# Filler products in the openings of two attentions, and a shorter first lot on GpSimd

## The chip, the cores and the metric

One NeuronCore of one Trainium2 chip. The metric is the device time of one execution of the program in microseconds; the time of a kernel is the median of several executions.

## What is computed

A block of two layers on 2048 tokens of 128 float32 numbers, `x` of shape (2, 1024, 128):

```python
x = x + attn0(layernorm(x))   # 16 heads of 8, 4 key/value heads, full attention over 1024, plus a state-space scan and a gated FFN
x = x + moe0(layernorm(x))    # 8 experts, 2 per token
x = x + attn1(layernorm(x))   # 16 heads on a shared latent of 32, causal over 1024
x = x + moe1(layernorm(x))    # integrator with shared and routed experts, 2 steps
...
scores = jnp.einsum('bhqd,bhkd->bhqk', q, k) / jnp.sqrt(jnp.float32(hd))
attn = jax.nn.softmax(scores, axis=-1)
attn = jnp.einsum('bhqk,bhkd->bhqd', attn, v)
```

Filler products write only into scratch banks of PSUM that are overwritten later, so they change no result.

## The kernel before, in words

One function, `attention` (line 141), builds both attentions. It is called with a "front" object that threads other work of its layer through it: `HybridFront` (line 642) for the first, a causal one for the second. The work is cut into 8 units of 4 heads and one batch each. For every unit two passes run over the scores:

- the **max pass**: 32 steps (`max_unit`, line 366) of 128 queries x one head. TensorE writes the scores of up to 1024 keys into two banks as bf16 quads, a quad (`quad`, line 359) being four products of 32 columns side by side, line 362. VectorE takes the row maximum (`take_max`, line 573: line 581 for the full, line 578 for the causal attention). Two pairs of banks alternate, so TensorE is at most two steps ahead of VectorE. In the causal attention the steps grow from 128 to 1024 keys.
- the **exp pass**: slots `s` (32 for the full, 24 for the causal attention), each with two exp quads (`exp_unit`, line 393), two exponentials on ScalarE (line 528) and, in every second slot, products with v (`pv_quad`, line 413, line 425).

Between them the maxima of half a unit are negated and split into three bf16 parts by five small operations on VectorE (`combine`, lines 591 to 595), turned on TensorE (`turn_max`, line 388), copied by ScalarE (`rows`, line 514) and sent by three DMAs on SyncE's queue into the operand of the exp quads (line 310). The exp pass of a unit runs in the same slots as the max pass of the next; a table computed from costs (`places`, lines 206 to 224) sets which max step stands in which half slot.

The first unit has nothing before it to share slots with. So `attention` begins with an **opening**: the first `own_from` max steps of unit 0 alone (21 in the full attention, 30 in the causal one), with the front's own products between them (`front.tensor_second`), the combine after step 15 on VectorE, the transposes `turn_max(0, 0)` after step 17 on TensorE, and then slot 0 of the body. To these steps TensorE adds fillers (`filler`, line 451): one bf16 quad of a 128x128 identity over 512 columns. In the full attention they follow steps 8 to 20, in the causal one steps 24 to 29, and eight more stand in slots 1 to 3 and 6 to 10 of the causal body.

Meanwhile GpSimd makes 96 products ahead for the scan that follows the first attention (`HybridFront.gpsimd_third`, line 743: the product of line 759, then its DMA, line 762). They come in lots: before product 7, 13, 19 and so on, GpSimd waits until the next combine of VectorE is done (`mparts_ready`).

In the trace, tiles bear the names of the memory they lie in: `banks` are PSUM banks, `attn_ka` and `attn_qa` the keys and queries, `attn_identb` the bf16 identity, `attn_mx` to `attn_mparts` the maxima and their parts. ScalarE's line 528 writes the probabilities, two of whose four buffers are borrowed and appear as `centred_squares`.

Of the kernel before, what the change touches and what calls it, by code (L numbers as in the profile page):

```python
# [140 lines left out]
def attention(k, tag, q_lin, k_lin, k_heads, v, causal, attn_t, front, units, tok=None, residual=False,  # L141
# [6 lines left out]
    nc = k.nc  # L148
# [11 lines left out]
    with ExitStack() as ctx:  # L160
# [18 lines left out]
        scores_exp = [k.bank[4], k.bank[5]]  # L179
        out_acc = k.bank[6]  # L180
        turned = k.bank[7]
# [25 lines left out]
        first_half = sum(1 for u in max_units if u[0] < QT // 2)  # L207
        joined = [COMBINE if causal and n in (first_half - 1, NM - 1) else 0 for n in range(NM)]
        whole = sum(cost) + sum(joined)
        own_from = min(n for n in range(NM + 1) if sum(cost[n:]) * reached[NE] <= sum(cost) * reached[DUE + 1])  # L210
        stream = [(0, n) for n in range(own_from, NM)] + [(1, n) for n in range(own_from)]
        places, done, spent = [], 0, 0
        for place in range(2 * NE):
            upto = done
            share = reached[place // 2] + weight[place // 2] * (1 + place % 2) / 2
            while upto < NM and spent + cost[stream[upto][1]] / 2 <= whole * share / reached[NE]:
                n = stream[upto][1]
# [24 lines left out]
        mrow_ready = [k.sem(f"{tag}_mrow_ready{h}") for h in range(2)]  # L242
# [26 lines left out]
        with nc.Block() as block:  # L269
# [85 lines left out]
            def _(pe):  # L355
# [3 lines left out]
                def quad(out, lhs, rhs, start=True):  # L359

                    for t in range(4):
                        last = nc.tensor.matmul(out[sl(t, 32), :], lhs[:, sl(t, 32)], rhs, start=start, stop=True,  # L362
                                                skip_group_check=True)
                    return last
# [48 lines left out]
                def pv_quad(i, kt_slot, vstage, part):  # L413

                    qb, kt, _, c0 = exp_units[kt_slot]
                    if part == 0:
                        pe.wait_ge(probs_ready, 2 * (NE * i + kt_slot + 2))
                        if kt_slot == 0:
                            pe.wait_ge(vstaged, i + 1)
                        if kt_slot == 0 or kt_slot == MID:  # L420
                            pe.wait_ge(osb_ready, 2 * i + qb)
                    mid = (c0 + BLK) // 2
                    cols = slice(c0, mid) if part == 0 else slice(mid, BLK)
                    for j in range(4):
                        last = nc.tensor.matmul(out_acc[32 * j:32 * j + 32, cols], vstage[:, kt, kj(j), :],  # L425
                                                probs[(kt_slot + j // 2) % 4][:, j % 2, cols],

                                                start=kt == 0 and part == 0,
                                                stop=kt_slot + 1 == half_end[qb], skip_group_check=True)
                    if part == 1:  # L430
                        last.then_inc(pv_done, 2)

                def turn_out(i, qb):

                    pe.wait_ge(osb_ready, 2 * i + qb + 1)
                    pe.wait_ge(normed, 2 * i + qb)

                    if qb == 0:
                        pe.wait_ge(mrow_ready[1], i + 1)
                    elif i + 1 < UNITS:  # L440
                        pe.wait_ge(mrow_ready[1 if causal else 0], i + 2)
                    for t in range(4):
                        last = quad(turned[:, sl(t, TILE)], osb[:, sl(t, TILE)], k.m("ident"))
                    last.then_inc(oturned, 1)

                def first_pass(i, place):
                    for ahead, n in places[place]:
                        if i + ahead < UNITS:
                            max_unit(i + ahead, n)

                def filler(bank):
                    quad(bank, ident_b[:, :], ident_b[:, :].unsqueeze(1).to_broadcast([128, 4, 128]))

                def body(i):
                    for s in range(NE):
                        odd = s % 2 == 1
                        if causal and i == 0 and s in (1, 2, 3, 6, 7, 8, 9, 10):
                            pe.wait_ge(mrow_ready[0 if s < 6 else 1], 1)
                            filler(turned[:, :])
                        if odd and s > 1:  # L460
                            products_with_v = (i, s - 3, vst[i % 2])
                        elif odd and i > 0:
                            products_with_v = (i - 1, NE - 2, vst[1 - i % 2])
                        else:
                            products_with_v = None
                        if products_with_v:
                            pv_quad(*products_with_v, 0)
                        exp_unit(i, s, (0,))
                        first_pass(i, 2 * s)
                        exp_unit(i, s, (1,))  # L470
                        if s == turn_at[1]:
                            turn_max(i, 1)
                        if s == turn_at[0] and i + 1 < UNITS:
                            turn_max(i + 1, 0)
                        first_pass(i, 2 * s + 1)
                        if products_with_v:
                            pv_quad(*products_with_v, 1)
                        if s == OUT_AT and i > 0:
                            turn_out(i - 1, 1)
                        if s == MID + 3:  # L480
                            turn_out(i, 0)
# [3 lines left out]
                for n in range(own_from):  # L485
                    max_unit(0, n)
                    front.tensor_second(pe, n)
                    if n >= (own_from - 6 if causal else 8):
                        filler(scores_exp[0][:, :])
                    if n == first_half + 1:  # L490
                        turn_max(0, 0)
                for i in range(UNITS):
# [149 lines left out]
class HybridFront:  # L642
# [100 lines left out]
    def gpsimd_third(self, pool):  # L743

        nc, scan = self.k.nc, self.scan
        pool.wait_ge(self.part_ready[0][2], 3)
        pool.wait_ge(self.part_ready[1][2], 3)
        n = 0
        for b in range(2):
            for jj in range(D // 16):  # L750
                for m in AHEAD_UNITS:
                    if n >= 7 and n % 6 == 1:
                        pool.wait_ge(self.mparts_ready[(n // 6 - 1) % 2], (n // 6 + 1) // 2)
                    channel = 32 * (m % 4) + 4 * jj + m // 4
                    stage, kept = self.stage[n % 2], self.kept[n % 2]
                    if n >= 2:
                        pool.wait_ge(kept, 16 * (n // 2))
                    x = scan.x_turned[:, 8 * b:8 * b + 8, channel:channel + 1].to_broadcast([128, 8, TILE])
                    nc.gpsimd.tensor_tensor(stage[:, :, :], scan.b_turned[:, 8 * b:8 * b + 8, :], x, ALU.mult)\  # L759
                        .then_inc(self.made_ahead, 1)  # L760
                    pool.wait_ge(self.made_ahead, n + 1)
                    pool.dma_start(self.d["ahead"][n], stage[:, :, :]).then_inc(kept, 16)
                    n += 1
        for i in range(2):
            pool.wait_ge(self.kept[i], 16 * (n // 2))
# [2479 lines left out]
```

## Time and profile before

| | before |
|---|---|
| median of 3 runs | 1913.61 us (1909.39 to 1915.45) |
| profiled execution | 1912.95 us |
| its span in the profile | 1911.1 us |
| mean granted clock of TensorE | 0.919 |
| TensorE matmul busy | 1649.7 us (86%) |
| VectorE busy | 1478.6 us (77%) |
| ScalarE busy | 1350.1 us (71%) |
| GpSimd busy | 888.5 us (46%) |

The span runs from the first to the last instruction on the core; the profiled execution's own time has 1.85 us more around it. The first attention with its front takes roughly the stretch from 60 to 520 us, its opening begins at 108; the scan with the first MoE follows; the second attention's opening begins near 1287. The granted clock is the share of TensorE's full clock, 2.4 GHz, that was given in a stretch: 1.00 is 2.4 GHz, 0.50 is 1.2 GHz, and a number between them is a mean over both. Durations of products in the trace include the way through the array after the last column, so the time from one start to the next is what a product costs on TensorE.

### The profile page before, as it was taken

How to read it: one execution, taken by the hardware profiler on the slowest of the kernel's cores; microseconds unless marked ns; L12 is line 12 of the kernel's file. 1: busy time of each engine (PE TensorE's matmuls, PEld its weight loads, DVE VectorE, ACT ScalarE, POOL GpSimd, SP SyncE). 2: the span in 40 equal slices, each digit the busy share in tenths (PEclk: the TensorE clock that was granted, in tenths of full speed). 3: DMA queues.
4: the chain of work that ended last, by engine and by line, in shares of the span. 5: the costliest groups of instructions: out<-in, count | busy, mean ns of one | idle time of the engine just before them, and what ended most of it. 6: DMA issues, size and time to landing. Idle time of an engine off the chain costs nothing. (4 is left out here: it accounts for less than half of the span.)

```text
span 1911.1 us, 45999 instructions
## 1 busy us (share of the span) xinstructions
PE 1649.7 (86%) x17410; PEld 874.4 (46%) x17422; DVE 1478.6 (77%) x1729; ACT 1350.1 (71%) x2673; POOL 888.5 (46%) x572
## 2 busy tenths in 40 slices
PE   6789999999788877777777669998999998999996
PEld 2235555555344444444444433433656556344442
DVE  3688899999299999999999975447888845556457
ACT  4417888888799999989999953443777773654443
POOL 1165666666099999999999981000000002000000
PEclk8858999999998888898888889996999999999998
DMA  2343444443489898888888942021222100000000
GB/s 117 123 160 139 157 154 161 159 153 141 141 312 315 314 315 298 311 279 292 302 322 296 305 150 88 12 73 42 47 37 45 29 4 18 1 1 0 0 6 17
DMA packets 82504, 278.86 MB, mean 146 GB/s; under 512 B 11159, under 2 KB 11954, under 8 KB 81311
## 3 DMA queue, kind: packets, MB, share of 16 engines
q1 hardware_dynamic: 68223, 225.67, 35.6%
q0 software_dynamic: 13824, 50.34, 6.8%
q8 instruction: 124, 2.03, 0.5%
q10 hardware_dynamic: 288, 0.45, 0.1%
q14 instruction: 45, 0.37, 0.1%
HBM read 214.72 MB, written 61.21 MB: 144 GB/s over the span
## 5 line engine op out<-in xcount | busy, mean ns | idle before, releaser
L1664 POOL TENSOR_TENSOR hc<-st,ct 128x1024 f32<-128x1024 f32 x256 | 598.2, 2374 | 8.2 <-DVE st L1623 7.7
L1623 DVE TENSOR_TENSOR_SCAN st<-da,banks 128x1024 f32<-128x1024 f32 x256 | 562.5, 2265 | 17.3 <-ACT da L1580 7.2
L528 ACT ACTIVATE attn_probs<-banks 128x512 f32<-128x512 f32 (+3 forms) x640 | 324.9, 534 | 93.3 <-PE banks L362 76.7
L362 PE MATMUL banks<-attn_qa,attn_ka 75*32 75x512 bf16 (+3 forms) x3584 | 347.9, 365 | 9.1 <-DMA attn_qa<-attn_mrow 2.8
L581 DVE TENSOR_REDUCE attn_mx<-banks 128x1 f32<-128x1024 f32 x256 | 309.8, 1223 | 32.7 <-PE banks L362 20.5
L1588 ACT ACTIVATE ut<-b_turned,mats 128x128 f32<-128x128 f32 x1024 | 311.7, 387 | 1.7
L362 PE MATMUL banks<-attn_ka,attn_qa 72*32 72x512 bf16 (+3 forms) x3584 | 291.3, 381 | 17.9 <-DVE attn_mx L578 11.0
L1580 ACT ACTIVATE da<-dt,mats 128x1024 f32<-128x1024 f32 x256 | 282.3, 1138 | 27.2 <-DVE st L1623 19.3
L1505 PE MATMUL banks<-hc,onecol 128*32 128x512 f32 x1024 | 159.5, 699 | 93.6 <-POOL onecol L1662 73.6
L759 POOL TENSOR_TENSOR made_ahead<-b_turned,x_turned 128x1024 f32<-128x1024 f32 x96 | 184.0, 1916 | 93.4 <-DVE attn_mparts L595 72.1
L578 DVE CUSTOM_DVE_ANT_0 banks<-banks,attn_maskwide 128x128 f32<-128x128 f32 (+7 forms) x256 | 191.1, 775 | 31.8 <-PE banks L362 28.4
L1481 PE MATMUL banks<-mats,ut 128*128 128x128 f32 x1024 | 177.4, 307 | 37.5 <-DVE st L1623 21.5
L425 PE MATMUL banks<-attn_probs,attn_vst 128*32 128x256 f32 (+3 forms) x2560 | 180.9, 350 | 1.6 <-ACT attn_probs L528 0.5
L528 ACT ACTIVATE centred_squares<-banks 128x512 f32<-128x512 f32 x256 | 150.6, 596 | 39.0 <-PE banks L362 29.5
L1481 PEld LDWEIGHTS banks<-mats,ut 128*128 128x128 f32 x1024 | 137.5, 154 | 80.4 <-ACT ut L1588 48.2
L362 PEld LDWEIGHTS banks<-attn_qa,attn_ka 75*32 75x32 bf16 x3584 | 101.5, 95 | 133.2 <-ACT attn_probs L528 47.6
L1489 PEld LDWEIGHTS banks<-mats,ua 128*128 128x128 f32 x768 | 104.7, 167 | 106.3 <-issue 66.9
L362 PEld LDWEIGHTS banks<-attn_ka,attn_qa 72*32 72x32 bf16 x3584 | 108.3, 99 | 98.1 <-DVE attn_mx L578 23.7
L2609 PE MATMUL banks<-hid_m,ew 128*128 128x512 f32 x320 | 146.5, 592 | 0.5
L1489 PE MATMUL banks<-mats,ua 128*128 128x128 f32 x768 | 131.0, 326 | 6.8 <-DVE st L1623 6.5
L3048 POOL MEMSET route_tok<- 128x128 bf16 x1 | 0.2, 204 | 274.5 <-issue 274.5
L425 PEld LDWEIGHTS banks<-attn_probs,attn_vst 128*32 128x32 f32 x2560 | 78.5, 110 | 34.3 <-issue 5.2
(445 smaller groups left out, 1953.3 us busy)
## 6 DMA issues: line engine op xcount, KB each, us to landing
dt<-dt_rows SPq DMA_DIRECT2D x256, 512.0 KB, 5.6
ahead<-made_ahead POOLq DMA_DIRECT2D x96, 512.0 KB, 3.5
ua<-ahead SPq DMA_DIRECT2D x96, 512.0 KB, 5.9
attn_qa<-q_lin SPq DMA_DIRECT2D x144, 64.0 KB
attn_ka<-k_lin SPq DMA_DIRECT2D x72, 64.0 KB
moe_w<-in_moe_w SPq DMA_DIRECT2D x2, 2048.0 KB, 9.8
mats<-in_mats SPq DMA_DIRECT2D x1, 2988.5 KB, 13.1
xparts_kept<-xparts_lin SPq DMA_DIRECT2D x3, 512.0 KB, 3.7
```

Of the source, the lines that this page charges most:

```text
L362: last = nc.tensor.matmul(out[sl(t, 32), :], lhs[:, sl(t, 32)], rhs, start=start, stop=True, skip_group_check=True)
L425: last = nc.tensor.matmul(out_acc[32 * j:32 * j + 32, cols], vstage[:, kt, kj(j), :], probs[(kt_slot + j // 2) % 4][:, j % 2, cols],  star ...
L528: nc.scalar.activation(probs[s % 4][:, jj, c0:BLK], scores_exp[jj][:, c0:BLK], ACT.Exp, scale=scale).then_inc(probs_ready, 1)
L578: nc.vector.tensor_tensor_reduce(out, out, mask_wide[:, SEQ - w:SEQ], 1.0, -BIG, ALU.add, ALU.max, mx[:, qt, j:j + 1]).then_inc(max_taken, 1)
L581: nc.vector.reduce_max(mx[:, qt, j:j + 1], out, AX.X).then_inc(max_taken, 1)
L759: nc.gpsimd.tensor_tensor(stage[:, :, :], scan.b_turned[:, 8 * b:8 * b + 8, :], x, ALU.mult)\
L1481: ins = nc.tensor.transpose(pair[:, i // 4, sl(i % 4, TILE)], buf[:, i, :], k.m("ident"))
L1489: ins = nc.tensor.transpose(pair[:, i // 4, sl(i % 4, TILE)], ua[q % 3][:, i, :], k.m("ident"))
L1580: nc.scalar.activation(da[n % 4][:, :], dt[n % 4][:, :], ACT.Exp, scale=a_now[:, g, jp:jp + 1])\
L1588: nc.scalar.activation(ut[TURNED.index(n) % 2][:, i, :], b_turned[:, 8 * b + i, :], ACT.Copy, scale=x_now[:, i, g, jp:jp + 1]).then_inc(ut ...
L1623: nc.vector.tensor_tensor_scan(st[n % 4][:, :], da[n % 4][:, :], pair[:, :, :].rearrange("p h t -> p (h t)"), 0.0, ALU.mult, ALU.add).then ...
L1664: nc.gpsimd.tensor_tensor(hc[n % 8][:, :], st[n % 4][:, :], ct[:, b * SEQ:(b + 1) * SEQ], ALU.mult)\
```

## The change

It has two parts.

*Fillers.* A new `wide_filler` is one float32 product: stationary the 128x128 identity, moving 256 columns (the identity twice), into one bank. In the first opening it follows each of the steps 1 to 20 (20 wide fillers), where before bf16 fillers followed steps 8 to 20 (13 of them); four more stand at the head of slots 0, 1, 2 and 4 of unit 0, behind a wait for ScalarE's first copy of the rows. In the second opening wide fillers follow the odd steps below 16 (8 of them) and all steps from 20 to 29 (10, behind the same kind of wait), where before bf16 fillers followed steps 24 to 29; the eight bf16 fillers of the causal body stay.

*GpSimd's lots.* The first lot has five products instead of seven, so each later lot begins two products earlier, and one more lot, of one product, stands at the end.

```diff
+                def wide_filler(bank):
+                    nc.tensor.matmul(bank[:, 0:256], k.m("ident"), k.m("ident").unsqueeze(1).to_broadcast([128, 2, 128]),
+                                     start=True, stop=True)
+
                 def body(i):
                     for s in range(NE):
                         odd = s % 2 == 1
                         if causal and i == 0 and s in (1, 2, 3, 6, 7, 8, 9, 10):
                             pe.wait_ge(mrow_ready[0 if s < 6 else 1], 1)
                             filler(turned[:, :])
+                        if not causal and i == 0 and s in (0, 1, 2, 4):
+                            pe.wait_ge(mrow_ready[0], 1)
+                            wide_filler(turned)
...
                 for n in range(own_from):
                     max_unit(0, n)
                     front.tensor_second(pe, n)
-                    if n >= (own_from - 6 if causal else 8):
-                        filler(scores_exp[0][:, :])
+                    if causal:
+                        if n < first_half and n % 2 == 1:
+                            wide_filler(turned)
+                        if n >= first_half + 4:
+                            pe.wait_ge(mrow_ready[0], 1)
+                            wide_filler(turned)
+                    elif n >= 1:
+                        wide_filler(scores_exp[0])
                     if n == first_half + 1:
                         turn_max(0, 0)
...
                 for m in AHEAD_UNITS:
-                    if n >= 7 and n % 6 == 1:
-                        pool.wait_ge(self.mparts_ready[(n // 6 - 1) % 2], (n // 6 + 1) // 2)
+                    if n >= 5 and n % 6 == 5:
+                        pool.wait_ge(self.mparts_ready[n // 6 % 2], n // 12 + 1)
```

Lines behind the new function are 13 higher than before.

The order of TensorE's instructions around the transposes of the first opening, before (`banks_1` and `banks_3` are the score banks of the max steps, `banks_5` those of the exp quads, `banks_7` the bank of the transposes; `x8` is two quads, that is one max step):

```order
L388 MATMUL banks_7<-attn_identb,attn_mparts 12x128 x4
L362 MATMUL banks_1<-attn_ka,attn_qa 32x512 x8
L362 MATMUL banks_5<-attn_identb 32x512 x4
L362 MATMUL banks_3<-attn_ka,attn_qa 32x512 x8
L362 MATMUL banks_5<-attn_identb 32x512 x4
L362 MATMUL banks_1<-attn_ka,attn_qa 32x512 x8
L362 MATMUL banks_5<-attn_identb 32x512 x4
L362 MATMUL banks_5<-attn_qa,attn_ka 32x512 x4
L362 MATMUL banks_3<-attn_ka,attn_qa 32x512 x8
L362 MATMUL banks_5<-attn_qa,attn_ka 32x512 x8
L362 MATMUL banks_1<-attn_ka,attn_qa 32x512 x8
```

and now:

```order
L388 MATMUL banks_7<-attn_identb,attn_mparts 12x128 x4
L362 MATMUL banks_1<-attn_ka,attn_qa 32x512 x8
L455 MATMUL banks_5<-mats 128x256
L362 MATMUL banks_3<-attn_ka,attn_qa 32x512 x8
L455 MATMUL banks_5<-mats 128x256
L362 MATMUL banks_1<-attn_ka,attn_qa 32x512 x8
L455 MATMUL banks_5<-mats 128x256
L455 MATMUL banks_7<-mats 128x256
L362 MATMUL banks_5<-attn_qa,attn_ka 32x512 x4
L362 MATMUL banks_3<-attn_ka,attn_qa 32x512 x8
L362 MATMUL banks_5<-attn_qa,attn_ka 32x512 x4
L455 MATMUL banks_7<-mats 128x256
```

A wide filler (line 455, on `mats`, where the float32 identity lies) stands in each place of a bf16 filler; one more stands in front of the first exp quad and one in front of slot 1, and slots 2 and 4 follow likewise. Ahead of this piece the wide fillers follow steps 1 to 7 too, where there was nothing.

TensorE in the second opening, from step 22 on, before:

```order
L362 MATMUL banks_1<-attn_ka,attn_qa 32x512 x4
L362 MATMUL banks_1<-attn_ka,attn_qa 32x256 x4
L362 MATMUL banks_3<-attn_ka,attn_qa 32x512 x4
L362 MATMUL banks_3<-attn_ka,attn_qa 32x256 x4
L362 MATMUL banks_1<-attn_ka,attn_qa 32x512 x4
L362 MATMUL banks_1<-attn_ka,attn_qa 32x384 x4
L362 MATMUL banks_5<-attn_identb 32x512 x4
L362 MATMUL banks_3<-attn_ka,attn_qa 32x512 x4
```

and now:

```order
L362 MATMUL banks_1<-attn_ka,attn_qa 32x512 x4
L362 MATMUL banks_1<-attn_ka,attn_qa 32x256 x4
L455 MATMUL banks_7<-mats 128x256
L362 MATMUL banks_3<-attn_ka,attn_qa 32x512 x4
L362 MATMUL banks_3<-attn_ka,attn_qa 32x256 x4
L455 MATMUL banks_7<-mats 128x256
L362 MATMUL banks_1<-attn_ka,attn_qa 32x512 x4
L362 MATMUL banks_1<-attn_ka,attn_qa 32x384 x4
```

The fillers begin four steps earlier, behind step 20, and each is one product on `banks_7` instead of four on `banks_5`.

GpSimd's products and DMAs where the second lot begins, with what they wait for, before (the row with two waits is the eighth product; the seven above it are the first lot, the last two of which stand here):

```order
L759 TENSOR_TENSOR made_ahead<-b_turned,x_turned 128x1024 [waits ahead_kept1]
L762 DMA ahead<-made_ahead 128x1024 [waits front_made_ahead]
L759 TENSOR_TENSOR made_ahead<-b_turned,x_turned 128x1024 [waits ahead_kept0]
L762 DMA ahead<-made_ahead 128x1024 [waits front_made_ahead]
L759 TENSOR_TENSOR made_ahead<-b_turned,x_turned 128x1024 [waits ahead_kept1,attn0_mparts_ready0]
L762 DMA ahead<-made_ahead 128x1024 [waits front_made_ahead]
```

and now (the row with two waits is the sixth product, the first lot has the five above it):

```order
L772 TENSOR_TENSOR made_ahead<-b_turned,x_turned 128x1024 [waits ahead_kept1]
L775 DMA ahead<-made_ahead 128x1024 [waits front_made_ahead]
L772 TENSOR_TENSOR made_ahead<-b_turned,x_turned 128x1024 [waits ahead_kept0]
L775 DMA ahead<-made_ahead 128x1024 [waits front_made_ahead]
L772 TENSOR_TENSOR made_ahead<-b_turned,x_turned 128x1024 [waits ahead_kept1,attn0_mparts_ready0]
L775 DMA ahead<-made_ahead 128x1024 [waits front_made_ahead]
```

The wait for the first combine has moved from the eighth product to the sixth; nothing else in GpSimd's order moved.

## Rows read from the trace of the kernel before

**Rows 1.** Busy time by stretch: from:to us, busy us (instructions) per engine, granted clock, DMA.

```profile
120.00:140.00 20.00, 15.73 (x148) 5.15 (x144) 19.39 (x22) 0.82 (x2) 16.96 (x13) 0.50 0.53 204
140.00:160.00 20.00, 20.00 (x228) 8.23 (x224) 12.34 (x11) 11.60 (x21) 10.65 (x9) 0.60 0.33 133
160.00:180.00 20.00, 19.45 (x376) 11.79 (x364) 18.14 (x22) 16.93 (x31) 12.66 (x11) 1.00 0.45 142
...
1280.00:1300.00 20.00, 14.00 (x79) 3.88 (x78) 12.89 (x38) 5.28 (x9) 0.00 (x0) 0.73 0.00 1
1300.00:1320.00 20.00, 16.70 (x148) 6.74 (x148) 14.82 (x35) 4.45 (x8) 4.58 (x4) 0.59 0.21 81
1320.00:1340.00 20.00, 19.95 (x408) 11.73 (x404) 15.41 (x52) 12.18 (x27) 0.00 (x0) 0.75 0.13 24
```

**Rows 2.** PE in order of time, first opening: start us, us, line, tiles, idle before.

```profile
108.25 1.90 PE L362 MATMUL banks<-attn_ka,attn_qa 72*32 72x512 bf16 x16
...
118.66 0.64 PE L362 MATMUL banks<-attn_identb 128*32 128x512 bf16 x4
119.09 1.07 PE L362 MATMUL banks<-attn_ka,attn_qa 72*32 72x512 bf16 x8
119.94 0.64 PE L362 MATMUL banks<-attn_identb 128*32 128x512 bf16 x4
...
134.62 0.59 PE L388 MATMUL banks<-attn_identb,attn_mparts 128*12 128x128 bf16 x4 [3.22 <-DVE attn_mparts L595]
...
139.69 0.65 PE L362 MATMUL banks<-attn_qa,attn_ka 75*32 75x512 bf16 x4
```

**Rows 3.** PE in order of time, second opening.

```profile
1296.56 0.62 PE L362 MATMUL banks<-attn_ka,attn_qa 72*32 72x512 bf16 x4
1297.11 2.07 PE L1838 MATMUL banks<-attn_t,mats 32*128 32x512 f32 x2
1299.11 1.04 PE L362 MATMUL banks<-attn_ka,attn_qa 72*32 72x512 bf16 x8
...
1305.21 2.08 PE L1845 MATMUL banks<-hn,lat_fold 128*128 128x512 f32 x2
1307.08 1.92 PE L1846 MATMUL banks<-hn,lat_wkv 128*128 128x512 f32 x2
1308.78 1.49 PE L1848 MATMUL banks<-lat_wkv,hn 128*128 128x128 f32 x8
```

**Rows 4.** DVE in order of time, first opening; last row: a later combine.

```profile
128.47 1.22 DVE L581 TENSOR_REDUCE attn_mx<-banks 128x1 f32<-128x1024 f32 x1
129.72 1.80 DVE L591 TENSOR_SCALAR attn_mneg<-attn_mx 128x16 f32<-128x16 f32 x1
...
131.97 2.38 DVE L594 CAST attn_mparts<-attn_mres 128x16 bf16<-128x16 f32 x1
134.39 0.17 DVE L595 TENSOR_TENSOR attn_mparts<-attn_mres,attn_mparts 128x16 bf16<-128x16 f32 x1
...
482.67 0.17 DVE L591 TENSOR_SCALAR attn_mneg<-attn_mx 128x16 f32<-128x16 f32 x1
```

**Rows 5.** POOL in order of time: products and DMA issues of the first opening.

```profile
126.74 1.90 POOL L759 TENSOR_TENSOR made_ahead<-b_turned,x_turned 128x1024 f32<-128x1024 f32 x1 [0.17 <-DMA ahead<-made_ahead]
...
129.56 1.92 POOL L759 TENSOR_TENSOR made_ahead<-b_turned,x_turned 128x1024 f32<-128x1024 f32 x1
...
132.40 1.92 POOL L759 TENSOR_TENSOR made_ahead<-b_turned,x_turned 128x1024 f32<-128x1024 f32 x1
...
163.10 1.90 POOL L759 TENSOR_TENSOR made_ahead<-b_turned,x_turned 128x1024 f32<-128x1024 f32 x1 [10.87 <-DVE attn_mparts L595]
```

**Rows 6.** ACT in order of time, first slots of the body.

```profile
140.39 0.60 ACT L528 ACTIVATE centred_squares<-banks 128x512 f32<-128x512 f32 x1 [4.56 <-PE banks L362]
...
156.44 1.19 ACT L528 ACTIVATE attn_probs<-banks 128x512 f32<-128x512 f32 x2 [0.53 <-PE banks L362]
157.75 2.50 ACT L528 ACTIVATE centred_squares<-banks 128x512 f32<-128x512 f32 x4
```

## The prediction

> **What bounds the kernel now.** I read the stretches of 20 us first, then the engines in order of time at the two openings. In the steady body of the first attention TensorE is busy 19.45 of 20 us at a granted clock of 1.00 [rows 1], so a delay or a gain in an opening is carried whole to the end of that attention, and the next stages follow. The change acts only in the two openings, where the clock is at the lower of its two levels (1.2 GHz; full is 2.4): 0.50 in 120 to 140 us, 0.60 in 140 to 160, and 0.59 and 0.75 in 1300 to 1340 [rows 1].
>
> In the first opening a max unit begins at 108.25; a unit is 0.85 us at 1.2 GHz (119.09 to 119.94) and a bf16 filler 0.43 (118.66 to 119.09) [rows 2]. Their sum, 1.28, is almost the 1.25 that VectorE needs for a take (128.47 to 129.72) [rows 4], so the two engines keep step and today's fillers are nearly free. Then TensorE stands idle 3.22 us before the transposes of line 388, which wait for the combine [rows 2]. That combine lasts from 129.72 to 134.56. Two of its five small operations took 1.80 and 2.38 us where the same operation took 0.17 at 482.67 [rows 4]. Both ended within 0.05 us of the end of a GpSimd product (129.56 and 132.40, 1.92 each) [rows 5]. The first exp quad starts at 139.69, 5.07 after the transposes [rows 2]; the exps then run at 1.2 GHz until 156.44 [rows 6].
>
> **The price of a wide filler.** No row shows a single 128x256 float32 product between two 32-column quads, so I bound it. Its stream: L1845 to L1846 is 1.87 for two passes of 512 columns, the start of which is dearer by 0.16 than L1846's (durations 2.08 and 1.92), thus 0.85 per 512 columns and 0.85 for two passes of 256 [rows 3]. Its switches: a quad of 0.43 is followed by L1838 after 0.55 (+0.12); from L1838 to the next quad it is 2.00 against the 1.71 of two undisturbed passes (+0.29) [rows 3]. Sum at 1.2 GHz: 0.85 + 0.41 = 1.26. The lower end is 0.85, if the switches hide; no row shows a full-width product hiding them, so I take 1.26. At full clock the stream halves to 0.43 and the switches lie between 0.21 and 0.41: about 0.74.
>
> **Does the clock rise?** This decides the sign. For: it rose while the full-width float32 products L1845, L1846 and L1848 ran back to back (0.59 over 1300 to 1320 mixes both levels) [rows 1, 3]. Against: from 118.66 to 130 TensorE ran units and full-array bf16 fillers with almost no gap, a third of the time in the fillers, and the clock stayed at 0.50; from 140 to 156 it was busy 20.00 of 20 us and rose only as the exps reached 156.44, when float32 products with v were in the mix [rows 1, 2, 6]. In the new opening a period is 0.85 of unit and 1.26 of wide, of which 0.41 streams nothing: per 2.11 us, 0.85 of full-array columns, 0.85 of the unit's 72 rows and 0.41 empty. The nearest row is the bf16 mixture, 0.43 of full array to 0.85 of unit with nothing empty, and it did not raise the clock. I take: it stays at 1.2 GHz through the first opening, and rises, as before, in the eighth slot or so.
>
> The Trainium skill ("TensorE: Matmul & The Clock Gate", section "Why this matters for your kernels") says that keeping TensorE busy without gaps is what brings the full clock; by it the wide fillers, which close every gap, would bring it at once, which is the first rival below. The trace does not agree with it as it stands: 140 to 156 had no gap and stayed low [rows 1, 6].
>
> **First opening, summed.** Unit 0, then units 1 to 17 each with a wide: 108.25 + 0.85 + 17 x 2.11 = 145.0, where the transposes can start, against 134.62. VectorE now waits for TensorE: its sixteenth take follows unit 15, whose quads end at 108.25 + 0.85 + 15 x 2.11 - 1.26 = 139.5; with 0.3 of hand-over and 1.25 it ends near 141, and the combine, five operations of 0.17 with their hand-overs, about 1.05, near 142. That is before 145, so **GpSimd's shorter lot gives nothing here**: the fifth product ended at 128.64 [rows 5], the sixth now waits for the combine, and what it saves (1.80 + 2.38 - 2 x 0.17 = 3.8) lies beside TensorE. The later lots move by two members and cost nothing: GpSimd already waited 10.87 before the second lot [rows 5], and the last product, now behind the combine at 482.67 [rows 4], is the last that the scan reads. Then the transposes (4 x 128 columns, 0.43), three units with wides (6.33) and the wide of slot 0 (1.26): 145.0 + 8.0 = 153.0 for the first exp quad, against 139.69: +13.3. The rows on SyncE's queue had 5.07 us before and have 8.0 now, so they are there; the new wait for the row copy in front of that wide is met, and what queues behind it waits for the landing anyway. Slots 1, 2 and 4 add 3 x 1.26 = 3.8, TensorE having no idle time there. Sum **+17.1**. With switches at half price (1.06 per wide): 17 x 0.20 + 3 x 0.20 + 4 x 0.20 less, +12.3; hidden wholly, +7.4.
>
> **Second opening.** Eight wides stand among units 0 to 15: 8 x 1.26 = 10.1 at most, beside 6.0 us of TensorE's idle time in 1280 to 1300 and 3.3 in 1300 to 1320 [rows 1]. Most is hidden; I estimate +2.5 (0 to 6), since the idle time is not all where they stand. After L1848, at the raised clock, units 20 to 29 with wides need 0.43 + 0.74 = 1.17 at most each, no more than a take. There the full clock is likely to hold, as it is TensorE half idle that lost it before, and the mean of 0.75 over 1320 to 1340, that is 10 us at 1.2 GHz with TensorE full [rows 1], becomes full clock. That halves some 9 us, of which ACT's 0.6 per exp [rows 6] leaves 3.5. Sum **-1**; ends -5, and +11 if the clock falls again and ten wides cost 1.26 each.
>
> **Forecast:** 1912.95 (the profiled execution: span 1911.1 and 1.85 around it; the median of the runs is 0.66 above it) + 17.1 - 1 = **1929**; own range 1915 to 1936.
>
> **Rivals.**
> 1. *The wides raise the clock early.* Float32 at full width may weigh otherwise than a bf16 group; no row excludes that. If it rises within the first few units and holds, unit and wide take 0.43 + 0.74 = 1.17, under a take's 1.25. VectorE sets the pace as before, the combine starts near 130 and the shorter lot pays its 3.8 in full. The fourteen exps from 140.39 to 156.44, 16.05 us, go at 0.625 each (four in 2.50 at 157.75) [rows 6]: 8.75 plus four wides of 0.74: -4.3. Two units at low clock cost 2 x 0.86 = 1.7. Sum -6.4, the second opening -4: **1902.5**, between 1898 and 1907. It decides from the unit at which the clock rises: each one at 1.2 GHz loses 2.11 - 1.25 = 0.86, so the gain of 8.1 is gone after nine, near 128 us.
> 2. *It rises between that and the transposes*: 0 to +8 in the first opening and -4 in the second, 1909 to 1917, about **1914**.
> 3. *The wides are nearly free and the clock stays*, so that only the lot acts. TensorE's 3.22 of idle time would be the gain, **1910**; but 0.85 + 0.85 is already 0.45 above a take for seventeen units, 7.7 us, which eats it. I give it no more than 0.03.
>
> **How the numbers follow.** Forecast 0.53, rival 1 0.33, rival 2 0.11, rival 3 0.03. Within 0.3% (5.7 us), about what a measurement of this kernel tells from no change, lie rivals 2 and 3 almost whole; the forecast's own low end touches that band, which the rest of rival 2 balances. So faster 0.33, same 0.13, slower 0.54. The range must take in rival 1 and most of the forecast: 1898 to 1934.
>
> **What would show it.** Right: the granted clock stays 0.50 from 108 to 153 us, unit and wide follow each other every 2.1 us, the transposes come near 145 without idle time of TensorE before them, all five operations of the combine take 0.2 us, and the clock is full from 1310. Wrong: a granted clock of 1.00 before 128 us, with takes 1.25 apart and the transposes near 131.

## The result and the profile after

The changed kernel takes 1928.93 us (median of 13 runs) against 1910.31 of the kernel before (13 runs): ratio **1.0102, 95% interval 1.0083 to 1.0121**. By the medians it is slower by 18.6 us. One of its 13 runs took 2634.93 us, at a mean granted clock of 0.554; the ratio leaves that run out, and the median of the other twelve is 1927.39. The profiled execution took 1932.9 us with a span of 1931.1, against 1911.1 before. The mean granted clock of the whole span, 0.925 against 0.919, does not show where the time went; the stretches do.

The stretches of 20 us (columns as in [rows 1]) show the first opening at 0.50 from end to end, and longer; the clock of the second opening is at 0.79 and 1.00 where it had been at 0.59 and 0.75 [rows 1], on stretches that now lie some 19 us later:

```profile
120.00:140.00 20.00, 20.00 (x99) 5.87 (x98) 12.06 (x14) 0.24 (x1) 8.90 (x8) 0.50 0.41 154
140.00:160.00 20.00, 20.00 (x106) 6.82 (x102) 10.91 (x14) 2.37 (x4) 11.95 (x9) 0.50 0.27 106
160.00:180.00 20.00, 20.00 (x192) 7.85 (x192) 9.45 (x8) 9.27 (x17) 3.11 (x3) 0.55 0.13 53
...
1320.00:1340.00 20.00, 19.29 (x149) 7.45 (x149) 15.30 (x36) 4.34 (x8) 4.58 (x4) 0.79 0.21 81
1340.00:1360.00 20.00, 19.32 (x474) 11.72 (x478) 17.93 (x61) 14.54 (x32) 0.00 (x0) 1.00 0.15 25
```

In the first two rows the profile shows no idle time of TensorE (a wide is shown 1.22 us long and the next product starts 1.15 after it, so durations overlap and a short stretch without a stream does not appear as idle), and VectorE has fallen from 19.39 [rows 1] to 12.06: TensorE now sets the pace, at the lower clock. TensorE in order of time, where [rows 2] stood:

```profile
110.62 1.90 PE L362 MATMUL banks<-attn_ka,attn_qa 72*32 72x512 bf16 x16
112.44 1.22 PE L455 MATMUL banks<-mats 128*128 128x256 f32 x2
113.59 1.04 PE L362 MATMUL banks<-attn_ka,attn_qa 72*32 72x512 bf16 x8
114.57 1.22 PE L455 MATMUL banks<-mats 128*128 128x256 f32 x2
...
146.47 1.22 PE L455 MATMUL banks<-mats 128*128 128x256 f32 x2
147.62 0.38 PE L388 MATMUL banks<-attn_identb,attn_mparts 128*12 128x128 bf16 x2
...
155.25 0.62 PE L362 MATMUL banks<-attn_qa,attn_ka 75*32 75x512 bf16 x4
```

From one wide filler to the next it is 2.13 us (112.44 to 114.57); the wide itself with its entry and first-pass price is 1.15 (112.44 to 113.59), and the step behind it takes 0.98 to the next wide in place of 0.85. The transposes stand at 147.62 without idle time before them, where they had waited 3.22 us. VectorE at the combine, where [rows 4] stood:

```profile
142.34 1.23 DVE L594 TENSOR_REDUCE attn_mx<-banks 128x1 f32<-128x1024 f32 x1 [0.90 <-PE banks L362]
143.60 0.17 DVE L604 TENSOR_SCALAR attn_mneg<-attn_mx 128x16 f32<-128x16 f32 x1
...
144.23 0.17 DVE L607 CAST attn_mparts<-attn_mres 128x16 bf16<-128x16 f32 x1
144.44 0.17 DVE L608 TENSOR_TENSOR attn_mparts<-attn_mres,attn_mparts 128x16 bf16<-128x16 f32 x1
```

The takes now wait 0.90 us each for TensorE. The combine has lost its two long operations (1.80 and 2.38, now 0.17 each), but it ends at 144.61, three microseconds ahead of the transposes that need it. ScalarE, where [rows 6] stood:

```profile
155.93 0.60 ACT L541 ACTIVATE centred_squares<-banks 128x512 f32<-128x512 f32 x1 [7.10 <-PE banks L362]
...
168.34 0.60 ACT L541 ACTIVATE centred_squares<-banks 128x512 f32<-128x512 f32 x1 [1.88 <-PE banks L362]
...
178.50 1.91 ACT L541 ACTIVATE centred_squares<-banks 128x512 f32<-128x512 f32 x3 [0.67 <-PE banks L362]
```

These are the first, the ninth and the seventeenth exp of the body. The ninth stood here in the kernel before:

```profile
148.98 0.60 ACT L528 ACTIVATE centred_squares<-banks 128x512 f32<-128x512 f32 x1 [0.61 <-PE banks L362]
```

The clock rises at 178.2, with the seventeenth; before it rose at 156.0, with the fifteenth [rows 6].

Where the 19.96 us between the two spans lie: the first step begins 2.36 later, which is not the change (nothing ahead of it is touched, and in the profiles of this study it begins anywhere from 108.25 to 111.60). From the first step to an exp of the second unit (exp 104; these numbers count from 0, and a unit has 64) it takes 131.54 us against 113.06: **+18.48**. From the first step of the second opening to its exp 40 (from 0 again) it takes 63.92 against 66.12: **-2.20**. The rest of the program is 1064.46 us between these two pieces and 559.25 behind them before, 1062.13 and 562.90 after, with the same instructions: -2.33 and +3.65, such as also lie between kernels that differ in the openings alone. Sum 2.36 + 18.48 - 2.20 - 2.33 + 3.65 = 19.96.

TensorE in the second opening: behind the full-width block of the latent's products the clock has risen, and the single wides keep it:

```profile
1324.72 2.07 PE L1858 MATMUL banks<-hn,lat_fold 128*128 128x512 f32 x2
...
1329.36 0.51 PE L362 MATMUL banks<-attn_ka,attn_qa 72*32 72x512 bf16 x8
1329.80 0.70 PE L455 MATMUL banks<-mats 128*128 128x256 f32 x2
1330.43 0.51 PE L362 MATMUL banks<-attn_ka,attn_qa 72*32 72x512 bf16 x8
```

A step of 768 keys with its wide takes 1.07 us here (1329.80 to 1330.87, the next wide), where the kernel before had fallen back to 1.2 GHz from 1313 to 1330. Earlier in this opening the single wides did not keep it: TensorE came in at full clock, and the clock fell at 1314.8, behind this wait:

```profile
1312.42 0.35 PE L362 MATMUL banks<-attn_ka,attn_qa 72*32 72x384 bf16 x4 [2.16 <-DVE attn_mx L591]
1312.70 0.70 PE L455 MATMUL banks<-mats 128*128 128x256 f32 x2
```

### The profile page after: what moved, and what is told of

Same layout as the page of the kernel before. It is cut to its first block and busy times, and to the rows that moved or that the text cites. A ratio compares the mean times of both kernels' runs of the same rounds, so it can differ in the third digit from the quotient of the medians.

```text
span 1931.1 us, 46028 instructions
## 1 busy us (share of the span) xinstructions
PE 1662.0 (86%) x17430; PEld 875.7 (45%) x17430; DVE 1476.2 (76%) x1729; ACT 1350.1 (70%) x2673; POOL 888.2 (46%) x572
## 5 line engine op out<-in xcount | busy, mean ns | idle before, releaser
L362 PE MATMUL banks<-attn_qa,attn_ka 75*32 75x512 bf16 (+3 forms) x3584 | 347.4, 364 | 10.9 <-DMA attn_qa<-attn_mrow 4.1
L362 PE MATMUL banks<-attn_ka,attn_qa 72*32 72x512 bf16 (+3 forms) x3584 | 285.8, 375 | 10.6 <-DVE attn_mx L591 6.4
L1494 PE MATMUL banks<-mats,ut 128*128 128x128 f32 x1024 | 163.3, 299 | 40.5 <-DVE st L1636 30.9
L1494 PEld LDWEIGHTS banks<-mats,ut 128*128 128x128 f32 x1024 | 131.7, 150 | 75.5 <-ACT ut L1601 48.7
```

The source lines that it names most:

```text
L1494: ins = nc.tensor.transpose(pair[:, i // 4, sl(i % 4, TILE)], buf[:, i, :], k.m("ident"))
```

## The experiments

The theory: a single wide product between two groups of 32-column products costs two switches, 0.4 us in which nothing streams, and so it makes the step dearer and does not raise the clock; everything else follows. The rivals: column groups beside the steps never raise it; the type decides; full width itself is at fault; GpSimd's lot matters. The ratios are to the kernel before, measured beside each experiment on the same chip; the experiments ran on three chips, so times are compared only where the text says that the chip is the same.

**1. Two bf16 groups in place of the wide product** (g_bf16). The stream is as long, 0.85 us at 1.2 GHz, without a switch.

```diff
 def wide_filler(bank):
-    nc.tensor.matmul(bank[:, 0:256], k.m("ident"), ident twice, start=True, stop=True)
+    for _ in range(2):
+        filler(bank[:, :])
```

> The changed kernel, but each wide filler is two bf16 groups of 32-column products over 512 columns: the same 0.85 us of stream at 1.2 GHz, with no switch to full width. Theory (the clock stayed low since 0.41 us of each 2.13 us streamed nothing): step and filler take 1.71 us, TensorE is without a gap, the granted clock becomes 1.00 within some 7 us of the first fillers and holds; the combine starts near 130 us after a first step at 108, the shorter lot pays its 3 us, and the time is 8 to 13 us under the kernel before (ratio 0.993 to 0.996). Rival A (bf16 groups beside the steps never raise it, as in the kernel before): a step and filler of 1.71 us for the whole opening, 7 us later in the first opening and about 3 more in the body, ratio 1.003 to 1.006. Rival B (float32 counts for more than bf16): as rival A here, but not in the float32 groups.

Measured: 0.9953 (0.9933 to 0.9974), 1898.31 us. TensorE in order of time, first opening:

```profile
113.28 1.07 PE L362 MATMUL banks<-attn_identb 128*32 128x512 bf16 x8
114.14 1.07 PE L362 MATMUL banks<-attn_ka,attn_qa 72*32 72x512 bf16 x8
...
116.70 0.76 PE L362 MATMUL banks<-attn_identb 128*32 128x512 bf16 x8
117.30 0.60 PE L362 MATMUL banks<-attn_ka,attn_qa 72*32 72x512 bf16 x8
117.73 0.60 PE L362 MATMUL banks<-attn_identb 128*32 128x512 bf16 x8
```

Step and filler follow each other without loss (113.28, 114.14); in the third filler the clock rises, at 117.0, 5.4 us behind the first step, and stays. The transposes come 22.17 us behind the first step, against 37.01 with the wides and 26.37 before. The expectation's rival A, that such groups never raise the clock, falls.

**2. One float32 group of 32-column products** (g_f32).

```diff
-    nc.tensor.matmul(bank[:, 0:256], k.m("ident"), ident twice, start=True, stop=True)
+    quad(bank[:, 0:256], k.m("ident"), ident twice)
```

> The changed kernel, but each wide filler is one group of four float32 products of 32 columns over 256 columns: the same type and the same 0.85 us of stream, with no switch to full width. Theory: as the bf16 groups, clock at 1.00 early in the first opening, ratio 0.993 to 0.996. Rival A (only full-width products raise it, as those of lines 1845 to 1848 did): clock at 0.50 through the first opening, ratio 1.003 to 1.006. Rival B (float32 counts for more): rises here and not with bf16 groups.

Measured: 0.9940 (0.9920 to 0.9961), 1897.77 us. TensorE in order of time:

```profile
114.00 1.07 PE L362 MATMUL banks<-mats 128*32 128x256 f32 x8
114.85 1.07 PE L362 MATMUL banks<-attn_ka,attn_qa 72*32 72x512 bf16 x8
115.71 1.07 PE L362 MATMUL banks<-mats 128*32 128x256 f32 x8
116.56 0.65 PE L362 MATMUL banks<-attn_ka,attn_qa 72*32 72x512 bf16 x8
```

The clock rises at 116.6, 6.0 us behind the first step, and the transposes come after 22.33. The two types do the same. A second measurement, with more rounds:

> The kernel with float32 groups of 32 columns once more, with more rounds, beside its variations. Theory: ratio 0.992 to 0.996, clock at 1.00 some 7 us behind the first step.

Again 0.9940 (0.9920 to 0.9960), 1897.49 us. This kernel is faster than the kernel before and than the changed one.

**3. Two bf16 products of full width** (w_bf16): the switches, with the other type.

```diff
-    nc.tensor.matmul(bank[:, 0:256], k.m("ident"), ident twice, start=True, stop=True)
+    for _ in range(2):
+        nc.tensor.matmul(bank[:, :], ident_b[:, :], ident_b four times, start=True, stop=True)
```

> The changed kernel, but each wide filler is two bf16 products of full width, 128x128 by 512 columns: the same stream of 0.85 us at 1.2 GHz and the same switches at both sides. Theory: the switches cost much the same as with float32, step and filler near 2.1 us (2.0 if the first pass's share of 0.16 belongs to float32), the clock stays at 0.50 and the time is that of the changed kernel within 5 us, ratio 1.006 to 1.011. Rival B (the type decides, float32 being too weak or too dear): the clock rises, ratio under 1.000.

Measured: 1.0035 (1.0010 to 1.0061), 1912.56 us, between the two answers and below the range that the theory gave. TensorE in order of time:

```profile
112.78 1.03 PE L456 MATMUL banks<-attn_identb 128*128 128x512 bf16 x2
113.75 1.04 PE L362 MATMUL banks<-attn_ka,attn_qa 72*32 72x512 bf16 x8
114.72 1.03 PE L456 MATMUL banks<-attn_identb 128*128 128x512 bf16 x2
...
150.04 1.86 PE L456 MATMUL banks<-attn_identb 128*128 128x512 bf16 x4
151.83 0.40 PE L362 MATMUL banks<-attn_qa,attn_ka 75*32 75x512 bf16 x4
```

Step and filler take 1.94 us: the switches cost 0.12 on either side (0.97 each for 0.85 of stream), and the 0.16 of the first pass is float32's. The clock stays at 0.50 for the whole opening, as the theory says; but it rises at 151.75, where two fillers stand in a row before the first exp quad, and the body runs at full clock from its first slot. That, and 20 steps at 0.19 us less, is the distance to the changed kernel.

**4. Four wides in a row behind steps 1 and 2, single ones behind the rest** (wide_start): full width, float32, but less switching at the start.

```diff
 elif n >= 1:
-    wide_filler(scores_exp[0])
+    for _ in range(4 if n <= 2 else 1):
+        wide_filler(scores_exp[0])
```

> The changed kernel, but after steps 1 and 2 of the first opening stand four wide fillers in a row instead of one; the single ones after steps 3 to 20 stay. Theory (it is the share of the time without a stream, not the full width or the type, that keeps the clock low; at full clock single wides are enough to hold it): the clock becomes 1.00 within 10 us of the first step and stays so; a step with its single wide then takes no longer than a take; 5 us are lost at the start, 11 us won later; ratio 0.994 to 0.998. Rival (full-width products between column groups never carry the clock): it rises during the eight and falls again within some us, or does not rise; ratio over 1.010.

TensorE in order of time:

```profile
110.87 3.78 PE L455 MATMUL banks<-mats 128*128 128x256 f32 x8
114.58 0.62 PE L362 MATMUL banks<-attn_ka,attn_qa 72*32 72x512 bf16 x8
115.13 1.99 PE L455 MATMUL banks<-mats 128*128 128x256 f32 x8
...
117.60 0.70 PE L455 MATMUL banks<-mats 128*128 128x256 f32 x2
118.23 0.61 PE L362 MATMUL banks<-attn_ka,attn_qa 72*32 72x512 bf16 x8
118.77 0.70 PE L455 MATMUL banks<-mats 128*128 128x256 f32 x2
```

The clock rises at 114.6, at the end of the first four, and the single wides then hold it through the opening and the body, at 1.17 us for step and wide (117.60 to 118.77). So full width carries the clock, and the change's own pattern of the first opening holds it here once it is up; in the change it did not raise it. The time is a miss: 1.0005 (0.9989 to 1.0021), not 0.994 to 0.998. In the profiled execution, 1902.53 us, the lowest of the ten, it is 107.2 us from the first step to exp 104, against 113.1 before. A clock that rises later in the other executions is not the likely reason: the mean granted clock of the whole span was 0.940 in the profiled one, 0.933 to 0.941 in all ten, and 0.916 to 0.931 in the kernel before on this chip. Part of the miss may lie in what it is compared with: experiment 9 has the first opening of before and the second of the change, and in its profile the same way takes 110.5 us. On the same chip its kernel took 1908.79 us and this one 1905.67, 3.1 less, with 3.3 less on that way. Why neither is under the kernel before stays open.

**5. Half the length, without a switch** (g_half).

```diff
-    quad(bank[:, 0:256], k.m("ident"), ident twice)
+    quad(bank[:, 0:128], k.m("ident"), k.m("ident"))
```

> The kernel with float32 groups of half the length: four products of 32 columns over 128 columns, 0.43 us at 1.2 GHz, everywhere. Theory (it takes enough stream, as the kernel before shows with bf16 fillers of the same 0.43): the clock stays at 0.50 in the first opening until the products with v, as in the kernel before; step and filler 1.28; with the shorter lot the time is 0 to 4 us under before, ratio 0.998 to 1.000. Rival (any float32 group raises it): clock at 1.00 early, ratio 0.992 to 0.996.

Measured: 0.9993 (0.9974 to 1.0013). TensorE in order of time:

```profile
113.57 0.64 PE L362 MATMUL banks<-mats 128*32 128x128 f32 x8
114.00 1.07 PE L362 MATMUL banks<-attn_ka,attn_qa 72*32 72x512 bf16 x8
114.85 0.64 PE L362 MATMUL banks<-mats 128*32 128x128 f32 x8
```

From 113.57 to 127.0 step follows filler without a gap, at 1.28 us (later the trace shows 0.39 and 0.23 us of idle time), and the clock stays at 0.50 until 148.7, among the products with v. So TensorE without gaps for 13 us did not raise it, in float32 as little as in the kernel before with bf16; with twice the filler it rose (experiments 1 and 2). Empty time is therefore not the whole account: here there was none, and half the filler.

**6. GpSimd's shorter lot alone** (lot5).

```diff
-                    if n >= 7 and n % 6 == 1:
-                        pool.wait_ge(self.mparts_ready[(n // 6 - 1) % 2], (n // 6 + 1) // 2)
+                    if n >= 5 and n % 6 == 5:
+                        pool.wait_ge(self.mparts_ready[n // 6 % 2], n // 12 + 1)
```

> The kernel before with GpSimd's shorter first lot alone. Theory (the combine on the path only while TensorE keeps step with VectorE, as it does in the kernel before): the five operations of the combine take 0.17 us each, the transposes start near 131.3 instead of 134.62, and the time falls by about 3 us (ratio 0.998 to 0.9985). Rival (the shorter lot gives nothing anywhere, because the copy and landing of the rows end later than TensorE's own work): the transposes come earlier, the first exp quad does not, ratio 1.000.

Measured: 0.9986 (0.9969 to 1.0004), 1906.21 us: at the upper edge of what the theory named, with an interval that also holds 1, so the time does not show the gain. VectorE in order of time:

```profile
130.88 0.17 DVE L591 TENSOR_SCALAR attn_mneg<-attn_mx 128x16 f32<-128x16 f32 x1
...
131.50 0.17 DVE L594 CAST attn_mparts<-attn_mres 128x16 bf16<-128x16 f32 x1
```

The transposes come 22.93 us behind the first step in place of 26.37, the first exp 28.85 in place of 32.13: -3.3, as the theory has it, and not the rival's zero. But how much the old lot costs differs from one execution to the next. In the profile of experiment 9, which has the old lot in the same opening, one operation of the combine is long and not two:

```profile
132.32 0.18 DVE L602 CAST attn_mparts<-attn_mneg 128x16 bf16<-128x16 f32 x1
132.53 2.44 DVE L603 TENSOR_TENSOR attn_mres<-attn_mneg,attn_mparts 128x16 f32<-128x16 f32 x1
```

There the transposes come after 24.82 us and the first exp after 30.59, and the shorter lot is worth 1.7. In the profiled execution of this experiment the clock rose only at 169.7, six slots later than before, with the same order of work, which hid the gain there. With the mixture of the kernel before that moment differs between profiles: it came 43.9 us behind the first step in experiment 9, 47.7 before and 60.3 here. What sets it no run shows.

**7. Seven products with the float32 groups** (g_f32_lot7), against experiment 2:

```diff
-                    if n >= 5 and n % 6 == 5:
-                        pool.wait_ge(self.mparts_ready[n // 6 % 2], n // 12 + 1)
+                    if n >= 7 and n % 6 == 1:
+                        pool.wait_ge(self.mparts_ready[(n // 6 - 1) % 2], (n // 6 + 1) // 2)
```

> The kernel with float32 groups, but GpSimd's first lot of seven products as before. Theory (at full clock VectorE sets the pace, so a combine stretched by products 6 and 7 is on the path): two of the combine's operations take about 1.9 us again, the transposes come some 3 us later behind the first step than the 22.3 us with five products, ratio 0.9935 to 0.998, 2 to 3 us above the kernel with five. Rival (TensorE's units and fillers cover it): the transposes come at the same place and the time is the same.

Measured: 0.9950 (0.9930 to 0.9971), 1898.85 us, 1.4 above its twin with five on the same chip; the intervals do not part them. TensorE, with the stretch that the combine leaves it idle, and 2 us windows of the same place:

```profile
133.42 0.39 PE L388 MATMUL banks<-attn_identb,attn_mparts 128*12 128x128 bf16 x4 [1.87 <-DVE attn_mparts L607]
134.68 1.05 PE L362 MATMUL banks<-attn_ka,attn_qa 72*32 72x512 bf16 x8 [0.87 <-DVE attn_mx L593]
```

```profile
132.00:134.00 2.00, 0.39 (x4) 0.20 (x4) 1.93 (x3) 0.15 (x1) 1.70 (x2) 1.00 0.43 176
134.00:136.00 2.00, 1.32 (x16) 0.57 (x20) 1.98 (x3) 0.42 (x1) 1.63 (x2) 0.64 0.65 264
...
142.00:144.00 2.00, 2.00 (x44) 0.99 (x36) 1.92 (x2) 1.79 (x3) 1.21 (x2) 1.00 0.32 129
```

One operation of the combine took 1.93 us, and the transposes came 1.2 us later (23.57 behind the first step), not 3: a miss in size. But more was lost in another way. The clock fell at 134.5 and came back at 141.4, and the first exp is 3.2 to 3.9 us later than in the two profiles with five products (31.47 against 27.60 and 28.27).

**8. The first opening's wides alone, with those of the first body's slots** (first_only), against the change, with the old lot as in experiment 7:

```diff
                     if causal:
-                        if n < first_half and n % 2 == 1:
-                            wide_filler(turned)
-                        if n >= first_half + 4:
-                            pe.wait_ge(mrow_ready[0], 1)
-                            wide_filler(turned)
+                        if n >= own_from - 6:
+                            filler(scores_exp[0][:, :])
```

> The kernel before with the wide fillers of the first opening and its body alone; GpSimd's lot of seven and the second opening as before. Theory (the loss is the first opening at 1.2 GHz, and the shorter lot is hidden there): from the first step to the first exp 45.3 us as in the changed kernel (32.1 before), clock at 0.50 until behind the fourth slot, products 6 and 7 of GpSimd harmless because the combine begins 10 us later. About 17 to 20 us above before, ratio 1.009 to 1.0105. Rival (the shorter lot matters, in the sense that without it the combine is stretched on the path): 3 us more than the changed kernel, ratio over 1.0115.

Measured: 1.0104 (1.0079 to 1.0129), 1927.59 us (four runs); 45.31 us from the first step to the first exp, the same as in the changed kernel. Within these intervals the whole loss is the first opening, and the lot changes nothing in it: all five operations of the combine take under 0.18 us here with the old lot too.

**9. The second opening's wides alone** (second_only), against the change, with the old lot and without the wides in the first body's slots:

```diff
-                    elif n >= 1:
-                        wide_filler(scores_exp[0])
+                    elif n >= 8:
+                        filler(scores_exp[0][:, :])
```

> The kernel before with the wide fillers of the second opening alone. Theory (there the full-width block of lines 1845 to 1848 raises the clock and the wide fillers from step 20 hold it): the fall of the clock at 1313 to 1330 us is gone; from the first step of that opening to its exp 40 it takes some 2 to 3 us less than the 66.1 of before, ratio 0.9985 to 0.999. Rival (no net gain, the eight odd fillers cost what the clock gives): ratio 1.000, the interval across 1.

Measured: 1.0007 (0.9984 to 1.0031), the value of the rival. In the profile the way from the first step of the second opening to its exp 40 takes 63.61 us against 66.12: 2.5 less, as the theory has it, and too little for the runs to show.

**10. No fillers in the first body** (g_f32_nobody, and once more nobody_again), against experiment 2:

```diff
-                        if not causal and i == 0 and s in (0, 1, 2, 4):
-                            pe.wait_ge(mrow_ready[0], 1)
-                            wide_filler(turned)
```

> The kernel with float32 groups of 32 columns as fillers, without the four fillers in slots 0, 1, 2 and 4 of the first body. Theory (at full clock the body's own products keep it; TensorE is the bound there): four times 0.43 us less, some 1 to 1.7 us under the kernel with them, ratio to before about 0.993 to 0.994. Rival (the first slots have no products with v and cannot hold the clock): it falls between the first exp quad and slot 4 and comes back later, ratio 0.996 or more.

> The same without the four fillers in the first body's slots, once more with more rounds. If these fillers only cost time at full clock: 1 to 1.7 us under the kernel with them; if they are needed to hold the clock in some executions: the same or more. Ratio to before 0.992 to 0.996.

Measured: 0.9959 (0.9939 to 0.9980) and 0.9954 (0.9934 to 0.9973), not under experiment 2 (0.9940, twice); on the chip where both were measured it took 1900.48 us against 1897.49. In both profiles the clock holds without them, and the seventeenth exp comes 0.3 to 1.1 us earlier behind the first step (38.19 and 38.07 against 38.52 and 39.20). The expected gain of 1 to 1.7 us is not there in the time, and why not stays open.

## Why the prediction was right, point by point

*The size* was right: 1929 forecast, 1928.93 measured. That it fits to a tenth is luck: the forecast added 16.1 us to a profiled execution that lay 2.6 over the median of the larger number of runs, the two profiled executions differ by 19.95 and the medians by 18.6, and two terms were off in opposite directions.

*The price of a wide*, 1.26 us by the sum of stream, entry, first pass and exit, was right: a step with its wide was forecast at 2.11 and takes 2.13. So was the price at full clock, which no row showed: forecast 1.17 for a step of 1024 keys with its wide, and 1.17 in experiment 4.

*The clock stays low* was right, and the ground for it held up. The row that decided it was the nearest one, the bf16 mixture that had not raised the clock, and the empty 0.41 us that made the wide mixture thinner, not denser. Experiments 1 and 2 keep the stream and take the switches away, the 0.41 us with them, and the clock rises in 6 us; experiment 3 keeps them with the other type, and it stays low. That full width as such is not at fault is shown by experiment 4, where four wides in a row raise it. What is not shown apart is the empty time from the alternation itself: no run puts column groups beside the steps with an idle time of 0.4 us between them. The changed kernel shows TensorE busy 20.00 of 20 us at 0.50, and in experiment 5 it runs for 13 us without a gap at 0.50 too. The rule of the Trainium skill ("TensorE: Matmul & The Clock Gate", section "Why this matters for your kernels"), that a TensorE kept busy without gaps gets the full clock, does not hold here as it stands.

*The first opening*: transposes forecast 36.75 us behind the first step (145.0 less 108.25), measured 37.01; first exp quad +13.3 us against before, measured 44.64 less 31.44, +13.2; the three wides in slots 1, 2 and 4 forecast +3.8, measured +3.8 (by the profiles' own times the ninth exp is 19.36 late, the first 15.54). The sum was 17.1 and came out 18.5: what it missed is that the clock rose one slot later, which cost 1.4 more. It had been set to come "as before, in the eighth slot or so".

*GpSimd's lot gives nothing here*: right (experiment 8), since the combine ends three microseconds ahead of the transposes. The sixth product waits 13 us for it, and no one waits for the product. The 3.8 that rival 1 gave it where TensorE does not cover it was read from one execution in which two operations were long; experiments 6 and 9 put it at 1.7 to 3.3 in the profiles, and no time shows it apart from the noise (experiments 6 and 7).

*The second opening*: -1 forecast, -2.2 in the profile. The single terms: the eight wides up to step 15 were put at +2.5 and cost 1.0 by the transposes (18.07 us behind the first step in place of 17.07); the gain from a clock that holds was put at 3.5 and is 2.9 between the first exp and exp 40. That the clock holds behind the full-width block was an argument, and is shown: it rises at 1328.5, 24.2 us behind the first step of this opening, and stays (before it rose after 23.9 and fell again 3.4 later).

*The rivals*: the first one, a clock that rises early, was worked out at 1902.5 and does not occur with this change. With another filler of the same stream it does (experiment 2), and gives 1897.49 beside 1908.44 for the kernel before on that chip: -10.9, where the rival had 1902.5 less 1912.95, -10.4. Its terms, the shorter lot, the exps at 0.63 us and 2 us lost at the start, were not measured one by one, and the lot's was too large, as above: it is the sums that agree.

## What to carry to other kernels

Give a filler that is to raise TensorE's clock the shape of its neighbours, or put several in a row: one wide product between groups of 32 columns lost 0.4 us to two switches in float32 and 0.24 in bf16, and here this turned a gain of 0.6% into a loss of 1.0%. Compare fillers by what streams per period, not by whether TensorE is busy, and look at the granted clock of the stretch before counting on it. When an engine off the path is to be relieved, first see whether its consumer is still waiting for it after the other half of the change.

## What the runs showed that was not expected

The same single wides that did not raise the clock (41 us at 0.50, from 112.4 to 153.3) held it once it was up (1.00 from 114.6 on, experiment 4). In the one profile of experiment 7, behind idle times of 1.87 and 0.87 us in the opening, the clock was lost for 7 us, and a combine lengthened by 1.9 us came with a first exp that was 3.2 to 3.9 later; the time of that kernel does not show it. The dearer first pass of a full-width product behind column groups, 0.16 us at 1.2 GHz, was there with float32 and not with bf16 (the filler takes 1.15 us in the change and 0.97 in experiment 3, for the same stream). And two fillers in a row in front of the first exp quad ended the low clock in bf16 (151.8) but not in float32 (the change, where they stand at 153.3 and the clock rises at 178.2); one profile of each is no proof that this is more than chance.
